# Vision tower on one core: the slot logits of both images in one block, the second half's statistics behind the scaled keys, the gate's second half in the third gap

## The chip, the cores and the metric

The kernel runs on one NeuronCore of a Trainium2 chip. The metric is the device time of one launch in microseconds, as the median of several launches. Everything is float32; many products are split by hand into a high and a low part of the faster 32-bit format and summed from three products.

## The reference

64 images of 224 x 224 x 3 are cut into 196 patches each and embedded into 192 features. Then come an attention without softmax and a mixture of 64 slot experts, each with a residual and a normalization:

```python
h = patches(x) @ W.T                                   # 64 x 196 x 192
q, k, v = silu(h @ Wq), silu(h @ Wk), silu(h @ Wv)     # 12 heads of 16
energy = (q @ k.T) * exp(log_slope * (n - m)) * (n >= m)
a = (energy @ v) * sigmoid(h @ Wg1 @ Wg2) @ Wo
h = layernorm(h + layernorm(a) * ln_w + ln_b)
xn = rms_norm(h) * norm_w
logits = (l2(slots) * scale) @ l2(xn).T                # 64 slots x 196 tokens
y = softmax_over_tokens(logits) @ xn                   # slot inputs
y = gelu(y @ fc1 + b1) @ fc2 + b2                      # each slot its own expert
out = layernorm(h + softmax_over_slots(logits).T @ y)
```

## The kernel before, in words

Images go through in 32 pairs (`NP`). Each engine has its own program, written out by hand; the order of its instructions is the order of the code, and semaphores join the engines. Three phases follow each other.

**Phase 1, the steps.** `step(i, c, d, e, f, more)` exists once for each engine and does four stages of four different pairs: embedding and attention of pair i; output product, first norm and residual of pair i-1 (flag c); second norm, scaled tokens, their transpose, logits and softmaxes of pair i-2 (d); slot inputs and combine weights of pair i-3 (e). Steps 4 to 30 are a hardware loop; 0 to 3 and 31 are written out. A pair is held as 4 token tiles of 98 rows: tiles 0 and 2 are the first halves of the two images, tiles 1 and 3 the second halves.

The attention of a step is a dialogue between TensorE and VectorE over four PSUM banks (2 to 5). TensorE's `scores(i, k)` (L1227) writes a third of the products of queries and keys; VectorE's `decay(i, k)` (L947) multiplies them by the decay into `p_sb` and frees the banks; only then can TensorE write the next third. `values(i, k)` (L1260) multiplies `p_sb` by the values. Between scores(0), scores(1), scores(2) and values(2) TensorE has three gaps, which hold other work: in the first, `token_features` (L1296, transposes of the scaled tokens `xn` of pair i-2, which must wait for `hb_sb` since they use the banks from which VectorE copies `hb`), `keys_turned` (L1234, L1235), `combine_turned` (L1289) and `slot_inputs_turned` (L1280, L1282); in the second, `gate` (L1173 and L1174: 128 features into bank 0, the other 64 into bank 1), `values(i, 0)`, `states` (L1243) and the logits of the first image of pair i-2; in the third, the logits of the second image, `values(i, 1)`, `carried` (L1274) and `logits_turned` (L1311). `logits(j, a)` (L1303) makes two products for image a: 96 rows, 64 columns of the array, those of slots 0 to 63 or 64 to 127 of the result. A float32 product is two records in the trace.

VectorE's order in a step (names of the helpers): gains and first norm of the first halves, `residual(i-1, 0)` (L883), `residual_statistics(i-1, 0)` (L889, L892), `cosine_scales`, then `first_norm`, `residual` and `residual_statistics` of the second halves, the low part of the gate's `zs` (L1011), `hb` (L1018: the turned h plus a bias), decay(0), the scaled keys `kts` (L1027), decay(1), `state` (L1033), decay(2), `gated(i, 0)` (L954: `og` from the gate's tanh and the PSUM sum), `slot_maxima` (`lneg`, L967), `shifted_logits` (L960, L962), `gated(i, 1)`, and the sums of the softmaxes.

ScalarE, after the SiLUs of keys, queries and values: the turned tokens `tokT` (L674), copies of the turned slot inputs and combine weights, the tanh of the gate's two parts (`gt`, L658 and L661), the rounding of the second half of the next x (`xh`, L597), a load of the exponential's table (L609), `logits_kept` (`Es`, L680), `slot_exponentials` (L710), `token_exponentials` (L715).

GpSimd: low parts of x and of the turned h (L440, L496), the powers of the norms, the scaled tokens `xn` (`unit_tokens`, L526), the scaled queries `qd`, the combine weights `Cn` (L533). The sync engine issues the loads and stores; after its last step it loads the weights of the first slots as soon as the memory under them is free.

**The passage** (`drain` on TensorE, the straight code behind `phase1` on the others) finishes pairs 29, 30 (`one`) and 31 (`last`): for each, token features, logits, transposes, softmaxes, slot inputs. It is a chain from engine to engine, and TensorE fills part of its waits with `idle_products(bank, count)` (L1129), products whose results nobody reads.

**Phase 2** runs 32 pairs of slots over six weight buffers; **phase 3** combines, adds the residual, normalizes and stores.

## Time and profile before

| | us |
|---|---|
| median of 3 runs | 1193.31 (1191.71 to 1193.66) |
| the profiled execution, its own time | 1190.01 |
| span of its trace | 1188.3 |
| TensorE busy in the span | 1076.5 (91%) |
| VectorE busy | 862.8 (73%) |
| ScalarE busy | 738.8 (62%) |
| GpSimd busy | 628.2 (53%) |
| mean granted TensorE clock | 0.954 of full speed |

Busy time of TensorE is modelled, since its products are pipelined: each record lasts until its result is written, while the next one already streams. What a product costs is thus read from the distance between the starts of neighbours, not from its own duration, and the share of busy time says little. The chain of waits is more use, and the timelines of all engines laid beside each other.

### The profile page before, as it was taken

What the parts mean: (1) busy time and instruction counts of PE and PEld (TensorE: products, weight loads), DVE (VectorE), ACT (ScalarE), POOL (GpSimd) and SP (SyncE); (2) the same over time, 40 slices, a digit from 0 to 9 for tenths busy, and PEclk for the clock granted to TensorE, in tenths of its full rate; (3) what the DMA queues carried; (4) which work ended last, traced back from release to release, by engine and by line L of the source; (5) the groups of instructions that cost most, each with busy time, mean ns of one, the idle gap of its engine ahead of it and who ended that gap; (6) DMA issues with size and microseconds to landing.
All of it is one profiled execution on the core that took longest, in us unless ns stands there. A gap on an engine that the chain in (4) does not pass through costs nothing.

```text
span 1188.3 us, 35236 instructions
## 1 busy us (share of the span) xinstructions
PE 1076.5 (91%) x13008; PEld 837.5 (70%) x13008; DVE 862.8 (73%) x2154; ACT 738.8 (62%) x1711; POOL 628.2 (53%) x967
## 2 busy tenths in 40 slices
PE   7799999999999999999999999999988999996653
PEld 6677788777777777877777778777765655554331
DVE  5878888888888888888888888888872222223996
ACT  6357777777777777777777777777753111110666
POOL 4556666666666665666666666566641000001664
PEclk9999999999999999999999999999999999998555
DMA  4511222111111122111111112211074999995885
GB/s 157 201 52 53 65 88 66 54 54 54 54 54 54 54 69 83 64 54 54 54 54 54 54 54 79 76 61 54 14 306 129 420 423 423 423 424 166 246 257 177
DMA packets 50994, 158.48 MB, mean 133 GB/s; under 512 B 5658, under 2 KB 31664, under 8 KB 38644
## 3 DMA queue, kind: packets, MB, share of 16 engines
q1 hardware_dynamic: 33352, 145.11, 33.3%
q10 hardware_dynamic: 17600, 12.78, 3.5%
q8 instruction: 30, 0.49, 0.2%
q14 instruction: 12, 0.10, 0.0%
HBM read 132.25 MB, written 25.62 MB: 133 GB/s over the span
## 4 chain that ended last, share of the span: by engine, by line
POOL 36%; issue 27%; PE 22%; DVE 10%; ACT 2%; DVEq 1%; DMA 1%; POOLq 1%; ACTq 0%; SPq 0%
POOL xl L440 14%; PE ps L1463 6%; POOL xn L526 5%; PE ps L1482 4%; POOL ra L517 4%; POOL hTl L496 4%; POOL rstd L507 2%; DVE res L1103 2%; POOL invn L500 2%; PE ps L1498 2%; DVE st L1109 2%; PE ps L1489 2%; POOL qd L477 1%; DVE p_sb L947 1%; PE ps L1227 1%
## 5 line engine op out<-in xcount | busy, mean ns | idle before, releaser
L947 DVE TENSOR_TENSOR p_sb<-ps,dec 98x1568 f32<-98x1568 f32 x96 | 171.6, 1788 | 64.2 <-PE ps L1227 64.1
L440 POOL TENSOR_TENSOR xl<-x_sb,xh 128x392 fp32r<-128x392 f32 x186 | 190.2, 1049 | 45.7 <-ACT xh L597 45.7
L496 POOL TENSOR_TENSOR hTl<-hT,hTh 128x392 fp32r<-128x392 f32 x64 | 66.3, 1035 | 146.3 <-ACT hTh L705 98.6
L763 ACT ACTIVATE hg<-ps 128x768 f32<-128x768 f32 x32 | 25.9, 810 | 144.3 <-PE ps L1489 144.3
L883 DVE SCALAR_TENSOR_TENSOR t<-t,rstd,hb 98x192 f32<-98x192 f32 x128 | 93.1, 767 | 15.9 <-POOL rstd L507 15.5
L1095 DVE COPY y2st<-ps 128x192 f32<-128x192 f32 x32 | 11.4, 357 | 120.5 <-PE ps L1463 120.5
L554 POOL CAST pickb<-pick 128x128 fp32r (+1 forms) x32 | 9.4, 293 | 150.4 <-PE ps L1489 150.4
L780 ACT ACTIVATE o_sb<-res,nb,rstd 98x192 f32<-98x192 f32 x128 | 59.6, 536 | 44.6 <-DVE nb L1118 44.0
L1260 PE MATMUL ps<-p_sb,vpad 98*32 98x98 f32 x3072 | 85.7, 252 | 1.5 <-DVE p_sb L947 1.5
L1260 PEld LDWEIGHTS ps<-p_sb,vpad 98*32 98x32 f32 x3072 | 64.7, 110 | 26.7 <-issue 26.7
L1513 PE MATMUL ps<-y2b,cbuf 64*98 64x192 f32 x256 | 49.4, 537 | 37.6 <-POOL y2b L567 37.6
L609 ACT ACT_TABLE_LOAD x60 | 77.0, 1283 | 1.1
L597 ACT ACTIVATE xh<-x_sb 128x1176 fp32r<-128x1176 f32 x64 | 75.4, 1180 | 1.9 <-DMA x_sb<-in_xT 1.2
L1133 PE MATMUL ps<-xl,wh 128*128 128x392 f32 x192 | 70.0, 365 | 3.4 <-POOL xl L444 3.3
L698 ACT ACTIVATE h<-t,mur,ra 98x192 f32<-98x192 f32 x128 | 59.7, 537 | 19.1 <-DVE mur L914 18.9
L1513 PEld LDWEIGHTS ps<-y2b,cbuf 64*98 64x98 f32 x256 | 32.6, 268 | 54.2 <-issue 43.0
L1463 PEld LDWEIGHTS ps<-w2v,hgT 128*64 128x64 f32 x768 | 52.3, 137 | 25.8 <-issue 18.5
L1463 PE MATMUL ps<-w2v,hgT 128*64 128x192 f32 x768 | 69.5, 330 | 1.0 <-DVE hgT L1089 1.0
L1227 PE MATMUL ps<-qA,kA 32*98 32x196 f32 x1024 | 59.6, 345 | 10.7 <-ACT vpad L686 7.5
L1211 PE MATMUL ps<-xl,whl 128*128 128x392 f32 x192 | 68.1, 355 | 0.0
L1133 PE MATMUL ps<-wvl,hTh 128*98 128x192 f32 x256 | 67.3, 263 | 0.2 <-DVE t L876 0.2
L533 POOL TENSOR_TENSOR Cn<-Ec,crec 98x256 f32<-98x256 f32 x32 | 20.6, 645 | 86.3 <-DVE crec L977 86.3
(228 smaller groups left out, 3449.0 us busy)
## 6 DMA issues: line engine op xcount, KB each, us to landing
x_sb<-in_xT SPq DMA_DIRECT2D x32, 1176.0 KB, 5.4
w1v<-in_fc SPq DMA_DIRECT2D x32, 1152.0 KB, 11.1
w2v<-in_fc SPq DMA_DIRECT2D x32, 1152.0 KB, 13.6
h_dram<-h SPq DMA_DIRECT2D x32, 294.0 KB
h2r<-h_dram SPq DMA_DIRECT2D x32, 294.0 KB
out<-o_sb ACTq DMA_DIRECT2D x32, 294.0 KB
comb_dram<-cst SPq DMA_DIRECT2D x32, 98.0 KB, 5.1
cbuf<-comb_dram SPq DMA_DIRECT2D x32, 98.0 KB, 3.8
```

The costliest lines, as they stand in the source:

```text
L440: pool.tensor_tensor(xl[:, k], x_sb[:, k], xh[:, k].bitcast(F32), ALU.subtract)\
L496: pool.tensor_tensor(hTl[:, k], hT[:, k], hTh[:, k].bitcast(F32), ALU.subtract).then_inc(hTl_rdy[k], 1)
L597: act.activation(xh[:, c], x_sb[:, c], ACT.Copy).then_inc(xh_rdy, 1)
L609: act.activation(warm[:, 1:2], warm[:, 0:1], func)
L883: dve.scalar_tensor_tensor(t2[0:T, t], t2[0:T, t], rstd1[:, t:t + 1], hb[0:T, t], ALU.mult, ALU.add).then_inc(t2_rdy, 1)
L947: dve.tensor_tensor(dst, src, rate.unsqueeze(2).to_broadcast([T, 4, 2, TOK]), ALU.mult)\
L1133: pe.matmul(out, hi, x_lo, start=start, stop=False)
L1211: pe.matmul(ps[:, 1, 0:PT], whl[:, k], xl[:, k], start=(k == 0), stop=False)
L1227: mm = pe.matmul(ps[0:T, SC_AT + r, mt * TOK:(mt + 1) * TOK].rearrange("p (b n) -> p b n", b=2), keys[rows, n], queries[rows, :, n], start ...
L1260: mm = pe.matmul(ps[32 * r:32 * r + 32, 6 + k // 2, at:at + T], vpad[:, 2 * a + mt, 32 * h:32 * h + 32], p_sb[:, k % 2, mt, (2 * r + odd) ...
L1463: mm = pe.matmul(ps[64 * s:64 * s + 64, 4 + n % 2, 0:D], hgT[:, k, at:at + 64], w2v[n][:, s, k], start=(k == 0), stop=(k == FJ - 1))
L1513: mm = pe.matmul(ps[0:T, 2 * n + a, k * D:(k + 1) * D], cbuf[64 * a:64 * a + 64, n, k * T:(k + 1) * T], y2b[64 * a:64 * a + 64, n, :], sta ...
```

## The change

Four things. In every step, TensorE makes both images' logits in one block in the second gap, the two images alternating; `lg_mm`, which releases ScalarE's copy, comes once, as before. The gate's second part moves from the second gap behind scores(2) into the third, and with it the waits for the bank that it writes. VectorE's statistics of the second halves move from ahead of `zs` and `hb` to behind the scaled keys. ScalarE's rounding of x and its copy of the logits now stand between the two tanh. In the passage, two of the four tiles of each pair's scaled tokens go to ScalarE (for `one`, beside GpSimd; for `last`, beside VectorE), several pieces change places, and the numbers of idle products change. The load of slot pair 2's weights waits for the gate instead of the scores.

```diff
@@ sync
             sp.wait_ge(qd_rdy, 2 * NP)
-            sp.wait_ge(sc_mm, 3 * NP)
+            sp.wait_ge(g_mm, 2 * NP)
             load_weights(2, 2)
@@ gpsimd
-            def unit_tokens(j):
+            def unit_tokens(j, tiles=range(4)):
...
-            unit_tokens(one)
+            unit_tokens(one, range(2))
@@ scalar, step
                 act.activation(gt[:, 0:PT], ps[:, 0, 0:PT], ACT.Tanh, scale=0.5).then_inc(g_sb, 1)
+                if more:
+                    round_x(i + 1, 1)
+                if d:
+                    logits_kept(i - 2)
                 act.wait_ge(g_mm, 2 * i + 2)
...
                 last.then_inc(g_sb, 1)
-                if more:
-                    round_x(i + 1, 1)
                 if d:
                     use_table(ACT.Exp)
-                    logits_kept(i - 2)
                     slot_exponentials(i - 2)
@@ scalar, passage
             combine_kept(one - 1, 1, True)
+            act.wait_ge(cosc_rdy, one + 1)
+            act.wait_ge(y_mm, one)
+            for t in range(2, 4):
+                act.activation(xn[0:T, t], gn[0:T, t], ACT.Copy, scale=cosc[:, t:t + 1]).then_inc(xn_rdy, 1)
             token_rows(one)
+            squares(last)
             logits_kept(one)
             slot_exponentials(one)
             token_exponentials(one)
-            squares(last)
+            act.wait_ge(cosc_rdy, NP)
+            for t in range(2, 4):
+                act.activation(hb[0:T, t], gn[0:T, t], ACT.Copy, scale=cosc[:, t:t + 1]).then_inc(xn_rdy, 1)
             slot_inputs_scaled(one)
             slot_inputs_kept(one, 5, 0)
             token_rows(last)
-            combine_kept(one, 4, True)
             logits_kept(last)
             slot_exponentials(last)
+            combine_kept(one, 4, True)
             token_exponentials(last)
@@ vector, step
                     residual(i - 1, 1)
-                    residual_statistics(i - 1, 1)
                 dve.wait_ge(zh_rdy, i + 1)
...
                                   ALU.mult).then_inc(kts_rdy, 1)
+                if c:
+                    residual_statistics(i - 1, 1)
                 decay(i, 1)
@@ vector, passage
+            cosine_scales(one, size)
             residual(last, 0)
-            cosine_scales(one, size)
             residual(last, 1)
...
             tokens(last)
+            token_norms(last)
             slot_maxima(one)
             shifted_logits(one)
             slot_sums(one)
-            token_norms(last)
+            cosine_scales(last, size_last)
             dispatch_scaled(one, size)
+            dve.wait_ge(cosc_rdy, NP)
+            for t in range(2):
+                dve.tensor_scalar(hb[0:T, t], gn[0:T, t], cosc[:, t:t + 1], None, ALU.mult).then_inc(xn_rdy, 1)
+            token_sums(one)
             mean_shifts(last)
-            token_sums(one)
-            cosine_scales(last, size_last)
-            dve.wait_ge(cosc_rdy, NP)
-            for t in range(4):
-                dve.tensor_scalar(hb[0:T, t], gn[0:T, t], cosc[:, t:t + 1], None, ALU.mult).then_inc(xn_rdy, 1)
@@ tensor
-            def logits(j, a):
+            def logits(j):
                 pe.wait_ge(tokT_sb, j + 1)
                 for k in range(2):
-                    mm = pe.matmul(ps[64 * a:64 * a + 64, 0, 0:TOK], slT[:, k, :], tokT[0:G, k, a * TOK:(a + 1) * TOK],
-                                   start=(k == 0), stop=(k == 1))
-                if a:
-                    mm.then_inc(lg_mm, 1)
+                    for a in range(2):
+                        mm = pe.matmul(ps[64 * a:64 * a + 64, 0, 0:TOK], slT[:, k, :],
+                                       tokT[0:G, k, a * TOK:(a + 1) * TOK], start=(k == 0), stop=(k == 1))
+                mm.then_inc(lg_mm, 1)
@@ tensor, step
                 pe.wait_ge(kts_rdy, i + 1)
+                gate(i, 0)
+                if d:
+                    pe.wait_ge(tokT_sb, i - 1)
+                values(i, 0)
+                states(i)
+                if d:
+                    pe.wait_ge(g_sb, 2 * i + 1)
+                    logits(i - 2)
+                scores(i, 2, c)
                 if e:
                     pe.wait_ge(yT_sb, 2 * i - 4)
                     pe.wait_ge(cb_sb, i - 2)
-                gate(i)
-                if d:
-                    pe.wait_ge(tokT_sb, i - 1)
-                values(i, 0)
-                states(i)
-                if d:
-                    pe.wait_ge(g_sb, 2 * i + 1)
-                    logits(i - 2, 0)
-                scores(i, 2, c)
-                if d:
-                    logits(i - 2, 1)
+                gate(i, 1)
                 carried_ready(i)
                 values(i, 1)
@@ tensor, drain
                 slot_inputs_turned(one, 5, 0)
+                idle_products(2, 2)
+                token_features(last, hb)
                 idle_products(2, 3)
-                token_features(last, hb)
-                idle_products(2, 4)
-                logits(last, 0)
-                logits(last, 1)
+                logits(last)
+                idle_products(2, 2)
                 combine_turned(one, 4)
                 pe.wait_ge(Lc_rdy, one + 1)
                 logits_turned(last)
-                idle_products(2, 6)
+                idle_products(2, 4)
                 dispatch_turned(last)
                 idle_products(2, 2)
                 slot_inputs(last, hb)
-                idle_products(2, 4)
+                idle_products(2, 3)
                 pe.wait_ge(yT_sb, 2 * last)
                 slot_inputs_turned(last, 5, 0)
-                idle_products(2, 6)
+                idle_products(2, 5)
```

TensorE's order in the loop, from scores(1) to values(2), before (L1227 scores, L1173 and L1174 gate, L1260 values, L1303 logits):

```order
L1227 MATMUL ps<-qA,kA 98x196 x8
L1381 REGISTER_ALU
L1173 MATMUL ps<-zs,gw 128x392
L1174 MATMUL ps<-zs,gw 64x392
L1260 MATMUL ps<-p_sb,vpad 32x98 x16
L1243 MATMUL ps<-vpad,kts 32x32 x12
L1303 MATMUL ps<-tokT,slT 64x196 x2
L1221 REGISTER_ALU
L1227 MATMUL ps<-qB,kB 98x196 x8
L1303 MATMUL ps<-tokT,slT 64x196 x2
L1260 MATMUL ps<-p_sb,vpad 32x98 x16
L1274 MATMUL ps<-qd,state 32x98 x8
```

The same stretch now (L1237 scores, L1184 gate, L1270 values, L1314 logits):

```order
L1237 MATMUL ps<-qA,kA 98x196 x8
L1184 MATMUL ps<-zs,gw 128x392
L1270 MATMUL ps<-p_sb,vpad 32x98 x16
L1253 MATMUL ps<-vpad,kts 32x32 x12
L1314 MATMUL ps<-tokT,slT 64x196 x4
L1231 REGISTER_ALU
L1237 MATMUL ps<-qB,kB 98x196 x8
L1400 REGISTER_ALU
L1184 MATMUL ps<-zs,gw 64x392
L1270 MATMUL ps<-p_sb,vpad 32x98 x16
L1284 MATMUL ps<-qd,state 32x98 x8
```

The second logits went up ahead of scores(2), the gate's part of 64 features went down behind it.

VectorE's order in the loop, from the second halves' residual to decay(1), before (L889 and L892 the statistics, L947 the decays):

```order
L883 SCALAR_TENSOR_TENSOR t<-t,rstd,hb 98x192 x2
L889 BN_STATS st<-t 98x6 x2
L892 BN_AGGR mv<-st 98x2 x2
L1011 TENSOR_TENSOR zs<-ps,zs 16x392
L1014 REGISTER_ALU
L1018 TENSOR_TENSOR hb<-ps,lnb 98x768
L942 ISA
L947 TENSOR_TENSOR p_sb<-ps,dec 98x4x2x196
L1027 TENSOR_TENSOR kts<-ps,kdec 98x384
L942 REGISTER_ALU
L947 TENSOR_TENSOR p_sb<-ps,dec 98x4x2x196
```

And now (L897 and L900 the statistics, L955 the decays):

```order
L891 SCALAR_TENSOR_TENSOR t<-t,rstd,hb 98x192 x2
L1018 TENSOR_TENSOR zs<-ps,zs 16x392
L1021 REGISTER_ALU
L1025 TENSOR_TENSOR hb<-ps,lnb 98x768
L950 ISA
L955 TENSOR_TENSOR p_sb<-ps,dec 98x4x2x196
L1034 TENSOR_TENSOR kts<-ps,kdec 98x384
L897 BN_STATS st<-t 98x6 x2
L900 BN_AGGR mv<-st 98x2 x2
L950 REGISTER_ALU
L955 TENSOR_TENSOR p_sb<-ps,dec 98x4x2x196
```

The statistics stand between the scaled keys and decay(1), where before nothing stood.

## Rows read from the trace of the kernel before

**Rows 1.** Stretches: us, busy us and instructions by engine, TensorE clock, DMA share, GB/s

```profile
60.00:866.00 806.00, 769.87 (x10335) 634.52 (x10334) 676.21 (x1612) 603.10 (x1425) 512.86 (x742) 1.00 0.17 58
866.00:912.00 46.00, 37.66 (x433) 28.93 (x433) 24.58 (x78) 21.62 (x63) 14.20 (x27) 0.96 0.59 229
```

**Rows 2.** Waits, 120 to 850 us: engine, line, releaser, us in all, times, longest

```profile
PE ps L1296 <- DVE hb L1018: 24.4, 27, 0.9
```

**Rows 3.** Timeline of TensorE in step 16: start, us, line, tiles, shape, count

```profile
459.26 0.92 PE L1227 MATMUL ps<-qA,kA 32*98 32x196 f32 x16 [0.23 <-ACT vpad L686]
...
462.78 0.92 PE L1227 MATMUL ps<-qA,kA 32*98 32x196 f32 x16
463.75 0.42 PE L1173 MATMUL ps<-zs,gw 80*128 80x392 f32 x1
...
464.27 0.89 PE L1260 MATMUL ps<-p_sb,vpad 98*32 98x98 f32 x32
...
465.28 0.88 PE L1303 MATMUL ps<-tokT,slT 96*64 96x196 f32 x4
466.08 0.92 PE L1227 MATMUL ps<-qB,kB 32*98 32x196 f32 x16
...
469.38 0.88 PE L1260 MATMUL ps<-p_sb,vpad 98*32 98x98 f32 x32
```

**Rows 4.** Timeline of VectorE in step 16; in brackets the idle time before

```profile
458.45 0.60 DVE L889 BATCH_NORM_STATS2 st<-t 98x6 f32<-98x192 f32 x2
459.13 0.25 DVE L892 BATCH_NORM_AGGREGATE mv<-st 98x2 f32<-98x6 f32 x2
...
460.88 1.78 DVE L947 TENSOR_TENSOR p_sb<-ps,dec 98x1568 f32<-98x1568 f32 x1
462.58 0.55 DVE L1027 TENSOR_TENSOR kts<-ps,kdec 98x384 f32<-98x384 f32 x1
463.77 1.79 DVE L947 TENSOR_TENSOR p_sb<-ps,dec 98x1568 f32<-98x1568 f32 x1 [0.64 <-PE ps L1227]
...
467.07 1.79 DVE L947 TENSOR_TENSOR p_sb<-ps,dec 98x1568 f32<-98x1568 f32 x1 [1.35 <-PE ps L1227]
469.17 0.56 DVE L954 SCALAR_TENSOR_TENSOR og<-gt,ps 128x392 f32<-128x392 f32 x1 [0.30 <-PE ps L1274]
```

**Rows 5.** Timeline of TensorE, last step and passage

```profile
863.57 0.92 PE L1227 MATMUL ps<-qA,kA 32*98 32x196 f32 x16 [0.23 <-ACT vpad L686]
...
872.91 0.89 PE L1260 MATMUL ps<-p_sb,vpad 98*32 98x98 f32 x32
...
885.08 0.88 PE L1296 MATMUL ps<-ident,xn 98*96 98x98 f32 x8 [2.98 <-POOL xn L526]
...
886.87 0.89 PE L1303 MATMUL ps<-tokT,slT 96*64 96x196 f32 x8
...
892.46 0.87 PE L1324 MATMUL ps<-xn,DT 98*64 98x192 f32 x8 [1.99 <-DVE DT L928]
...
896.18 1.28 PE L1296 MATMUL ps<-ident,hb 98*96 98x98 f32 x8
...
900.38 0.40 PE L1311 MATMUL ps<-ident,Es 128*98 128x128 f32 x2 [0.80 <-ACT Es L680]
```

**Rows 6.** Timeline of VectorE, last step and passage

```profile
864.55 1.79 DVE L947 TENSOR_TENSOR p_sb<-ps,dec 98x1568 f32<-98x1568 f32 x1
...
891.48 0.16 DVE L906 TENSOR_TENSOR nra<-ss,ra 98x4 f32<-98x4 f32 x1 [1.80 <-ACT ysq L691]
```

**Rows 7.** Timeline of ScalarE in step 16

```profile
464.66 0.65 ACT L661 ACTIVATE gt<-ps 64x196 f32<-64x196 f32 x2
465.34 1.18 ACT L597 ACTIVATE xh<-x_sb 128x1176 fp32r<-128x1176 f32 x1
466.54 1.28 ACT L609 ACT_TABLE_LOAD   x1
...
470.03 0.46 ACT L710 ACTIVATE Es<-Es,lneg 128x196 f32<-128x196 f32 x1 [1.78 <-DVE lneg L967]
```

More of the change, by code:

```diff
@@ L524, in unit_tokens @@
                     pool.wait_ge(y_mm, j)
-                for t in range(4):
+                for t in tiles:
                     pool.tensor_tensor(xn[0:T, t], gn[0:T, t], cosc[:, t:t + 1].to_broadcast([T, D]), ALU.mult)\
@@ L1070, in _ @@
             slot_sums(one)
-            token_norms(last)
+            cosine_scales(last, size_last)
             dispatch_scaled(one, size)
+            dve.wait_ge(cosc_rdy, NP)
+            for t in range(2):
+                dve.tensor_scalar(hb[0:T, t], gn[0:T, t], cosc[:, t:t + 1], None, ALU.mult).then_inc(xn_rdy, 1)
+            token_sums(one)
             mean_shifts(last)
-            token_sums(one)
-            cosine_scales(last, size_last)
-            dve.wait_ge(cosc_rdy, NP)
-            for t in range(4):
-                dve.tensor_scalar(hb[0:T, t], gn[0:T, t], cosc[:, t:t + 1], None, ALU.mult).then_inc(xn_rdy, 1)
             slot_maxima(last)
@@ L1168, in rows_of_v, with gate @@
                 mm.then_inc(v_mm, 1)
-            def gate(i):
-                pe.wait_ge(q_sb, 2 * i + 2)
-                pe.wait_ge(zl_rdy, i + 1)
-                pe.matmul(ps[:, 0, 0:PT], gw[:, 0:DA], zs[:, :], start=True, stop=True).then_inc(g_mm, 1)
-                pe.matmul(ps[0:DB, 1, 0:PT], gw[:, DA:D], zs[:, :], start=True, stop=True).then_inc(g_mm, 1)
+            def gate(i, g):
+                if g == 0:
+                    pe.wait_ge(q_sb, 2 * i + 2)
+                    pe.wait_ge(zl_rdy, i + 1)
+                m = (slice(0, DA), slice(DA, D))[g]
+                pe.matmul(ps[0:m.stop - m.start, g, 0:PT], gw[:, m], zs[:, :], start=True, stop=True).then_inc(g_mm, 1)
             def slots_turned():
@@ L1379, in step @@
                 pe.wait_ge(kts_rdy, i + 1)
-                if e:
-                    pe.wait_ge(yT_sb, 2 * i - 4)
-                    pe.wait_ge(cb_sb, i - 2)
-                gate(i)
+                gate(i, 0)
                 if d:
@@ L1389, in step @@
                     pe.wait_ge(g_sb, 2 * i + 1)
-                    logits(i - 2, 0)
+                    logits(i - 2)
                 scores(i, 2, c)
-                if d:
-                    logits(i - 2, 1)
+                if e:
+                    pe.wait_ge(yT_sb, 2 * i - 4)
+                    pe.wait_ge(cb_sb, i - 2)
+                gate(i, 1)
                 carried_ready(i)
@@ L1416, in drain @@
                 idle_products(0, 4)
-                logits(one, 0)
-                logits(one, 1)
+                logits(one)
                 pe.wait_ge(t1_rdy, 4 * NP)
```

## The prediction

> **What bounds the kernel now.** I read the stretches first [rows 1]. The pipelined steps (60 to 866 us) take two thirds of the time, and there TensorE has work in flight for 770 of 806 us; in the passage from the steps to the slot products (866 to 912) for only 38 of 46 us. A step takes 26.95 us: the first scores of two steps 15 apart start at 459.26 and 863.57 [rows 3, 5]. TensorE is thus nearly the bound of a step, but a row of the timeline hides stalls, so the waits come next [rows 2]: TensorE waits 0.9 us in each of 27 steps for `hb`, VectorE's copy of the turned h, before it can turn the token features.
>
> Then the timelines of one step. I follow the distance from the first scores, scores(0), to the last values product, values(2), since everything that the change touches in a step lies between them: 469.38 - 459.26 = 10.12 us [rows 3]. In that stretch TensorE and VectorE hand one PSUM area back and forth: scores(0), decay(0), scores(1), decay(1), scores(2), decay(2), values(2). A decay takes 1.79 us, starts 0.99 after its scores (466.08 to 467.07), and TensorE goes on 0.12 after its end (460.88 + 1.78 = 462.66, scores(1) at 462.78) [rows 3, 4]. Other products fill the three gaps. The reader should see two delays there. First, decay(0) starts 460.88 - 459.26 = 1.62 after scores(0), not 0.99, because `hb` and the statistics of the second half (458.45 to 459.38, 0.96 with the gap to the next instruction) stand ahead of it. Second, in the third gap TensorE is late, not VectorE: decay(2) ends at 467.07 + 1.79 = 468.86, values(2) could start at 468.98 and starts at 469.38 [rows 3, 4].
>
> The last step is a natural experiment. There VectorE is in time: decay(0) starts 864.55 - 863.57 = 0.98 after scores(0), and values(2) follows at 872.91 - 863.57 = 9.34 [rows 5, 6].
>
> **The statistics behind the scaled keys.** They leave the place ahead of decay(0), so I take the last step's 0.98: decay(0) starts 0.64 earlier, and the 0.9 us wait for `hb` goes, since `hb` would be written at about the time that the first scores end. scores(1) then starts at 0.98 + 1.79 + 0.12 = 2.89 after scores(0). What VectorE does not do there it does after the keys: 462.58 + 0.55, then 0.96, so decay(1) starts at about 464.1 instead of 463.77 on the old clock, in place of an idle time of 0.64 [rows 4]. It ends at 465.9 and TensorE may go on at 466.0.
>
> **The second gap.** On TensorE the gate's second half leaves (the pair takes 464.27 - 463.75 = 0.52, a half 0.26) and the second image's logits arrive. One image's logits take 466.08 - 465.28 = 0.80 [rows 3]. What do both take in one block? The passage shows it: eight records in 0.89, where one image's four take 0.88 [rows 3, 5]. So the second image costs nothing beside the first, and I take 0.80. The block then runs 465.02 to 465.82, just ahead of the 466.0 at which VectorE lets scores(2) start. From scores(1) to scores(2) it is 466.0 - 462.78 = 3.22, before 3.30. VectorE, no longer TensorE, ends this gap, by 0.2 us, and this is what is late next.
>
> The Trainium skill ("TensorE: Matmul & The Clock Gate", Part 3, the mechanism) says that a weight load overlaps a running matmul only when it targets other rows of the array. Both images' logits use the same 96 rows and differ in columns, so by that rule they would run one after the other. The row of the passage speaks against it, with eight records in the time of four. The same row says that the alternation itself is worth nothing: there the images already stand one after the other and still overlap.
>
> **The third gap.** TensorE loses 0.80 of logits and gains 0.26 of gate. values(2) is then bound by decay(2): 0.99 + 1.79 + 0.12 = 2.90 after scores(2), before 3.30. TensorE's own work there sums to 3.30 - 0.80 + 0.26 = 2.76, which fits by 0.14.
>
> The sum of a step: 2.89 + 3.22 + 2.90 = 9.01, against 10.12, so 1.11 saved. Of it goes 0.09: VectorE's gating, and with it all that feeds the next step (logits shifted, means, second norm), started 0.21 ahead of values(2) (469.17 and 469.38) and will start 0.12 ahead; that chain is the one that VectorE and ScalarE work through without idle time afterwards. Net 1.02. For 29 steps that is 29.6 us, and the last step, already at 9.34, gives 0.33. **Steps: -29.9 us.**
>
> ScalarE's side is costed at nothing. Its second tanh now waits for the gate half behind scores(2). On the old clock the half starts at 466.0 + 0.9; the tanh starts 0.65 after its half (463.75 + 0.26 and 464.66) and takes 0.65, so it ends near 468.2, and table load and warming, 1.5, end at 469.7 [rows 3, 7]. Today the exponential behind them waits 1.78 for `lneg` and starts at 470.03; with the gating at 468.8 instead of 469.17 it could start at 469.65. So this wait is the cover, and it shrinks to nothing. The rounding of x (1.18) moves ahead of the tanh, into the time in which scores(2) runs. On GpSimd the token scales wait for the moved statistics about 1 us longer; the second split of x behind them, which waits for ScalarE's rounding today, starts no later than now. No DMA of the steps is moved.
>
> **The passage.** Four pieces. (1) TensorE waited 2.98 for GpSimd's four scaled tiles [rows 5]; now it does two and ScalarE two, and the scales come ahead of the residuals. The first logits come 1.4 us earlier, but ScalarE's squares of the last pair now stand between them and their copy, and take back about 1.0. (2) VectorE waited 1.80 for those squares before it could scale the dispatch weights [rows 6]; they are now done before, and the slot inputs (892.46) come 1.8 earlier instead, which includes piece (1). (3) The last pair's token features started 3.72 after the slot inputs (896.18) [rows 5]; with the scaled rows written by two engines beforehand, no wait is left but that for the turned slot inputs, 2.4 us: -1.3. (4) From these features to the turned logits it takes 900.38 - 896.18 = 4.20, with a 0.80 wait for ScalarE's copy, which stood behind another pair's combine copy [rows 5]; without that copy in front, and with fewer idle products, 3.4: -0.8. Fewer idle products (4 for 6, 3 for 4, 5 for 6) free the last chain by another 0.9. Together -4.8 us; bounds are -2 (only piece 2) and -6.5 (if every removed idle product and every slow product counts). The weights for the first slots are asked for in the last step and land long before the passage ends, so the third one's new wait (for the gate instead of the scores) costs nothing; the slot products keep their pace and just begin earlier. **Passage: -4.8 us.**
>
> **The sum** against the profiled execution: 1190.01 - 29.9 - 4.8 = 1155.3 us. The median of the three runs, 1193.31, lies 3.3 above that execution; for a median I predict 1193.31 - 34.7 = 1158.6 us, a ratio of 0.971. A difference under 0.2% (2.4 us) I count as no change.
>
> **Rivals.**
> (a) *The tail binds.* The chain gating, shifted logits, exponential, means, second norm takes the place of the removed wait, because ScalarE's slack before its exponential is down to nothing and VectorE's tail has none. If it holds back half a microsecond of each step, 15 us are lost: 1173 us. For it: the small slacks above. Against: TensorE has the whole first embedding block between values(2) and the first product that needs the result. Chance 0.17.
> (b) *Both images' logits do not overlap in the loop.* The joined block takes 1.61. It ends at 466.63, scores(2) starts 0.55 later than now, values(2) at 9.65 instead of 10.12 after scores(0): 0.47 a step less the 0.09. 30 steps give 11, the passage 4.8: 1177 us. That is the time that the skill's rule on rows would give. Against it: the passage's row. Chance 0.05.
> (c) *More than forecast.* The chain from decay to values loses a little more in each gap, and the passage gives its upper bound: 1150 us. Chance 0.10.
> (d) *Slower.* The second tanh is the mechanism. It stands behind the rounding of x and behind the copy of the joined logits, and TensorE's turning of the logits waits for it, with values(2) queued behind in TensorE's order. TensorE comes to that turning at about 468.4, and with the 0.14 that its gap has to spare, the tanh may end 0.3 us later than the 468.2 worked out before values(2) is late. The 1.02 of a step and the passage's 4.8 (0.16 a step) are used up from 1.5 us on; at 2.0 us the kernel loses 30 x 0.5 = 15 us: 1208 us. For it: it is the one operation that moves 2 us later in the step. Against: the rounding needs 1.18 and the copy one short row, and both fit into the 2.9 us between its two tanh. Chance 0.03.
> (e) *It does not do what it says.* The alternation adds nothing (which I expect), and VectorE comes out as the end of the second gap, so that only the moved statistics pay: about 9.34 as in the last step, 0.78 a step, 1165 us. Chance 0.10.
>
> **How the numbers follow.** The forecast itself, 1154 to 1163, has 0.55. The likeliest case gives the time. The range leaves out (d), (b) and the ends of (a) and (c): 1151 to 1173. Faster by more than 0.2%: 0.96; within 0.2%: 0.01, out of (a) at twice its price; slower: 0.03, which is (d).
>
> **What would show it.** In the changed profile: no wait of the token features' turning for `hb`; decay(0), (1), (2) at 0.98, 4.2 and 7.1 us after scores(0); values(2) at 9.0; one block of eight logits records in 0.9 us; a step of 25.9 us; ScalarE's wait before the exponential down from 1.8 to a few tenths; the passage near 41 us; slot products and output untouched. Wrong would be a step above 26.3 us, a logits block of 1.6 us, or a new wait on `gt` ahead of TensorE's turning of the logits.

## The result, and the profile after

| | before | changed |
|---|---|---|
| median, us | 1192.51 (1189.90 to 1193.66, 4 runs) | 1144.17 (1142.75 to 1145.80, 4 runs) |
| profiled execution, its span | 1190.01, 1188.3 | 1145.80, 1144.0 |
| ratio | | 0.960, 95% interval 0.958 to 0.962 |

The change saves 48 us. I had forecast 35 us and a range of 1151 to 1173 us; the result is below the range.

One step of the changed kernel on TensorE, from the first scores (L1237) to those of the next step: L1306 token features, L1184 gate, L1270 values, L1314 logits. It answers to [rows 3]:

```profile
441.47 0.92 PE L1237 MATMUL ps<-qA,kA 32*98 32x196 f32 x16 [0.23 <-ACT vpad L687]
442.52 0.87 PE L1306 MATMUL ps<-ident,xn 98*96 98x98 f32 x8
...
444.29 0.92 PE L1237 MATMUL ps<-qA,kA 32*98 32x196 f32 x16
445.14 0.45 PE L1184 MATMUL ps<-zs,gw 80*128 80x392 f32 x1
445.52 0.89 PE L1270 MATMUL ps<-p_sb,vpad 98*32 98x98 f32 x32
...
446.52 0.88 PE L1314 MATMUL ps<-tokT,slT 96*64 96x196 f32 x8
447.34 0.92 PE L1237 MATMUL ps<-qB,kB 32*98 32x196 f32 x16
448.19 0.39 PE L1184 MATMUL ps<-zs,gw 80*64 80x392 f32 x1
448.51 0.89 PE L1270 MATMUL ps<-p_sb,vpad 98*32 98x98 f32 x32
...
450.17 0.89 PE L1270 MATMUL ps<-p_sb,vpad 98*32 98x98 f32 x32
...
466.99 0.92 PE L1237 MATMUL ps<-qA,kA 32*98 32x196 f32 x16 [0.23 <-ACT vpad L687]
```

VectorE in the same step, L1025 the copy `hb`, L955 the decays, L897 the moved statistics, L962 the gating. It answers to [rows 4]:

```profile
441.43 0.96 DVE L1025 TENSOR_TENSOR hb<-ps,lnb 98x768 f32<-98x768 f32 x1
442.45 1.79 DVE L955 TENSOR_TENSOR p_sb<-ps,dec 98x1568 f32<-98x1568 f32 x1
...
444.62 0.61 DVE L897 BATCH_NORM_STATS2 st<-t 98x6 f32<-98x192 f32 x2
...
445.47 1.77 DVE L955 TENSOR_TENSOR p_sb<-ps,dec 98x1568 f32<-98x1568 f32 x1
...
448.33 1.79 DVE L955 TENSOR_TENSOR p_sb<-ps,dec 98x1568 f32<-98x1568 f32 x1 [0.93 <-PE ps L1237]
450.03 0.55 DVE L962 SCALAR_TENSOR_TENSOR og<-gt,ps 128x392 f32<-128x392 f32 x1
```

A step is 25.52 us long (466.99 - 441.47), 1.42 less than before. The token features follow the scores with no wait for `hb`. From scores(0) it is 2.82 us to scores(1), 5.87 to scores(2) and 8.70 to values(2); before it was 3.52, 6.82 and 10.12. From values(2) to the next scores(0) it is 16.82 us, as before (26.95 - 10.12 = 16.83). So the whole gain of a step is where the change is.

The logits of both images take 0.82 us in one block of eight records (446.52 to 447.34). The two halves of the gate take 0.38 (445.14 to 445.52) and 0.32 (448.19 to 448.51) apart, where the pair took 0.52.

ScalarE's second tanh (L665) and the exponential (L711), in the same step:

```profile
448.62 0.67 ACT L665 ACTIVATE gt<-ps 64x196 f32<-64x196 f32 x2 [0.83 <-PE ps L1184]
...
450.89 0.46 ACT L711 ACTIVATE Es<-Es,lneg 128x196 f32<-128x196 f32 x1
```

The exponential no longer waits at all (no bracket; before 1.78 [rows 7]), and the second tanh waits 0.8 us for its half of the gate. Nobody waits for it.

The last step and the passage on TensorE, which answers to [rows 5]: first scores, values(2), slot inputs of `one`, token features and turned logits of `last`; below it ScalarE's first GELU.

```profile
824.36 0.92 PE L1237 MATMUL ps<-qA,kA 32*98 32x196 f32 x16 [0.24 <-ACT vpad L687]
...
833.23 0.89 PE L1270 MATMUL ps<-p_sb,vpad 98*32 98x98 f32 x32
...
851.18 0.87 PE L1334 MATMUL ps<-xn,DT 98*64 98x192 f32 x8
...
853.71 0.84 PE L1306 MATMUL ps<-ident,hb 98*96 98x98 f32 x8
...
856.99 0.38 PE L1321 MATMUL ps<-ident,Es 128*98 128x128 f32 x2
```

```profile
866.29 0.81 ACT L771 ACTIVATE hg<-ps 128x768 f32<-128x768 f32 x1
```

Counted from the last step's scores(0), before and now: values(2) at 9.34 and 8.87; slot inputs at 28.89 and 26.82; token features of `last` at 32.61 and 29.35; turned logits at 36.81 and 32.63; GELU at 47.0 and 41.9. From the GELU to the end it is 277.7 us in both traces. Of the 5.1 us gained up to the GELU, 0.47 are the last step's (9.34 and 8.87) and 4.6 the passage's.

Not all of these 4.6 us come from the order of the work. In the trace before, TensorE's granted clock was at half speed in one stretch of the passage (the columns are those of [rows 1]):

```profile
893.70:897.10 3.40, 3.40 (x20) 2.98 (x19) 1.07 (x6) 0.66 (x3) 0.01 (x1) 0.50 0.05 18
```

In the changed kernel's trace it is 1.00 from the last step to the GELU. What such a stretch costs can be estimated from c1_stats below, which has the passage of before and a second stretch of 3.4 us at 0.50 in it: its GELU comes 48.7 us after the last step's scores(0), against 47.0. By this estimate some 1.7 of the 4.6 us are the clock's. All three traces with the old passage have such a stretch ahead of the GELU (before, c1_stats, c2_logits), and none of the nine with the new one. So it may well be an effect of the change, but no run separates it from the rest.

The balance of the two traces: the 29 periods between the first scores of steps 2 and 31 took 781.2 us and take 740.6, 40.6 less; last step and passage 5.1 less; the start, up to the first scores of step 2, takes 1.4 us more (82.3 and 83.7). Together 44.3, the difference of the spans. The medians differ by 48.3, since the profiled execution of before was one of its fastest and that of the changed kernel its slowest.

### The profile page after: what moved, and what is told of

The parts are those of the page before. It is cut to its first block, busy times and chain, and to the rows that moved or that the text cites. A ratio compares the mean times of both kernels' runs of the same rounds, so it can differ in the third digit from the quotient of the medians.

```text
span 1144.0 us, 35221 instructions
## 1 busy us (share of the span) xinstructions
PE 1059.4 (93%) x13000; PEld 826.5 (72%) x13000; DVE 859.9 (75%) x2152; ACT 745.1 (65%) x1715; POOL 629.4 (55%) x965
## 4 chain that ended last, share of the span: by engine, by line
POOL 37%; issue 25%; PE 20%; DVE 10%; DMA 3%; ACT 1%; DVEq 1%; POOLq 1%; ACTq 0%; SPq 0%
POOL xl L440 14%; PE ps L1471 5%; POOL xn L526 5%; POOL hTl L496 4%; PE ps L1490 4%; POOL ra L517 3%; POOL rstd L507 3%; POOL invn L500 2%; DVE res L1112 2%; DVE st L1118 2%; DMA w2v<-in_fc 2%; PE ps L1506 2%; PE ps L1497 2%; POOL qd L477 1%; POOL qd L481 1%
## 5 line engine op out<-in xcount | busy, mean ns | idle before, releaser
L955 DVE TENSOR_TENSOR p_sb<-ps,dec 98x1568 f32<-98x1568 f32 x96 | 171.3, 1784 | 33.3 <-PE ps L1237 31.6
L1270 PE MATMUL ps<-p_sb,vpad 98*32 98x98 f32 x3072 | 86.9, 254 | 0.8 <-DVE p_sb L955 0.5
L1270 PEld LDWEIGHTS ps<-p_sb,vpad 98*32 98x32 f32 x3072 | 65.7, 111 | 19.8 <-issue 14.4
L1237 PE MATMUL ps<-qA,kA 32*98 32x196 f32 x1024 | 59.6, 345 | 11.3 <-ACT vpad L687 7.5
L1144 PE MATMUL ps<-xh,wh 128*128 128x392 f32 x192 | 66.5, 346 | 0.0
```

The costliest lines, as they stand in the source:

```text
L955: dve.tensor_tensor(dst, src, rate.unsqueeze(2).to_broadcast([T, 4, 2, TOK]), ALU.mult)\
L1144: return pe.matmul(out, hi, x_hi, start=False, stop=stop)
L1270: mm = pe.matmul(ps[32 * r:32 * r + 32, 6 + k // 2, at:at + T], vpad[:, 2 * a + mt, 32 * h:32 * h + 32], p_sb[:, k % 2, mt, (2 * r + odd) ...
```

## The experiments

All ratios are against the kernel before on the same chip in the same rounds (medians 1192.1 to 1192.5).

### The parts of the change one at a time

**c1_stats**, the kernel before with only the statistics moved:

```diff
                     residual(i - 1, 1)
-                    residual_statistics(i - 1, 1)
...
                                   ALU.mult).then_inc(kts_rdy, 1)
+                if c:
+                    residual_statistics(i - 1, 1)
```

> Kernel before with one part alone: the statistics of the second halves behind the scaled keys. Theory (TensorE's own work fills gaps two and three, VectorE's lateness only the first): scores(1) comes 2.82 us after scores(0) instead of 3.52, both later gaps stay at 3.30, values(2) at 9.42 instead of 10.12, a step of 26.25 us, the kernel 20 us faster (about 1172). Rival (the statistics cost VectorE what they gain, and the whole gain of the change is the logits): within 3 us of before. Rival (the statistics alone bring the last step's 9.34): 26.17 us a step, 1170.

Measured: 1170.00 us, ratio 0.981 (0.978 to 0.985). The scores and the last values of one step on TensorE:

```profile
447.27 0.92 PE L1228 MATMUL ps<-qA,kA 32*98 32x196 f32 x16 [0.24 <-ACT vpad L686]
...
450.10 0.92 PE L1228 MATMUL ps<-qA,kA 32*98 32x196 f32 x16
...
453.31 0.92 PE L1228 MATMUL ps<-qB,kB 32*98 32x196 f32 x16
...
456.62 0.88 PE L1261 MATMUL ps<-p_sb,vpad 98*32 98x98 f32 x32
```

values(2) comes 9.35 us after scores(0), and a step takes 26.17 us: 0.78 saved. That is the last step's distance in the kernel before [rows 5, 6], to a hundredth, as the last rival said, and not the 9.42 of my theory. The gap from scores(1) to scores(2) is 3.21 here, not 3.30, and the row of the gate says why:

```profile
450.97 0.43 PE L1174 MATMUL ps<-zs,gw 80*128 80x392 f32 x1
```

It starts 0.87 after scores(1), where before it started 0.97 after (463.75 and 462.78 [rows 3]). Ahead of the gate stand waits for ScalarE's copies of the turned slot inputs and combine weights; with the token features no longer late, these copies come in time. The last step had been the better witness than my sum.

**c2_logits**, everything of the steps but the statistics, with the passage of before:

```diff
@@ against the changed kernel: vector, step
                     residual(i - 1, 1)
+                    residual_statistics(i - 1, 1)
...
-                if c:
-                    residual_statistics(i - 1, 1)
@@ all engines: the passage as before
```

> The other part of the steps alone: logits in one block, gate's second half in the third gap, ScalarE's order as in the change; statistics and passage as before. Theory: the first gap stays (scores(1) at 3.52), the second takes 3.05, the third 2.83 as in the changed kernel, values(2) at 9.40, a step of 26.2 us, the kernel 21 us faster (about 1171); with the statistics' 0.70 this makes the 1.42 a step of the change. Rival (the two parts need each other, since the second gap is VectorE's): under 0.4 us a step, 1181 or more.

Measured: 1173.79 us, ratio 0.985 (0.981 to 0.988).

```profile
449.69 0.92 PE L1229 MATMUL ps<-qA,kA 32*98 32x196 f32 x16 [0.23 <-ACT vpad L687]
...
453.28 0.92 PE L1229 MATMUL ps<-qA,kA 32*98 32x196 f32 x16
...
456.32 0.92 PE L1229 MATMUL ps<-qB,kB 32*98 32x196 f32 x16
...
459.16 0.88 PE L1262 MATMUL ps<-p_sb,vpad 98*32 98x98 f32 x32
```

A step takes 26.29 us, 0.66 saved. The second gap is 3.04 and the third 2.84, as forecast; the first gap grew by 0.07, to 3.59. Both parts pay alone, and 0.78 + 0.66 = 1.44 comes close to the 1.42 of the change. That the sum fits so well is in part chance: the earlier start of the gate (0.10 in c1_stats, 0.12 here, where its waits have moved away) is in both parts and counts once in the change, while the 0.07 lost in the first gap is in this part only.

**c3_passage**, the steps of before with the passage of the change:

```diff
@@ pool, scalar, vector, tensor: the passage as in the change
-            unit_tokens(one)
+            unit_tokens(one, range(2))
...
```

> Steps of the kernel before, passage of the change. Theory: 4.6 us faster, all of it between the last step's values and the first GELU; steps untouched at 26.95 us. Rival (a part of the passage's gain needs the changed last step): 3 us or less.

Measured: 1185.85 us, ratio 0.994 (0.992 to 0.995). In the traces the steps keep 26.95 us and the first GELU comes 42.4 us after the last step's scores, before 47.0: 4.6 saved, as expected. The medians say 6.4, and the interval 5.6 to 9.5, while the two profiled executions differ by only 2.3 (1190.01 and 1187.73): in this one, the slowest of its kernel, the clock was at 0.51 from 907.0 to 910.4, just behind the GELU, and from the GELU to the end it took 280.1 us instead of 277.7. With such stretches at half speed in some executions and not in others, a difference of 1 to 2 us between medians and trace can't be placed. The medians of the three parts, 22.2 + 18.4 + 6.4 = 47.0, come near the 48.3 of the whole.

### What the alternation is worth

**c4_order**, the changed kernel with the images one after the other inside the block:

```diff
-                for k in range(2):
-                    for a in range(2):
+                for a in range(2):
+                    for k in range(2):
                         mm = pe.matmul(ps[64 * a:64 * a + 64, 0, 0:TOK], slT[:, k, :],
```

> The changed kernel with the logits of the two images one after the other inside the block, not alternating. Theory (the images overlap in either order, as they did in the passage before): the block stays at 0.82 us, the kernel within 1.5 us of the changed one (1144). Rival (only alternating neighbours overlap, the rule that a weight load overlaps a product only on other rows of the array): the block takes 1.2 to 1.6 us, 0.4 to 0.8 us a step, 1156 to 1168.

Measured: 1143.87 us, ratio 0.960 (0.956 to 0.963), the time of the changed kernel. The block of logits and the scores behind it:

```profile
442.31 0.89 PE L1314 MATMUL ps<-tokT,slT 96*64 96x196 f32 x8
443.13 0.92 PE L1237 MATMUL ps<-qB,kB 32*98 32x196 f32 x16
```

It takes 0.82 us in this order too. The gain comes from putting the images' logits side by side in the queue, whatever their order in it. Both use the same 96 rows of the array and different columns. So here four products, eight records, with their weight loads on two sets of columns take 0.82 us, where one image's two products, four records, took 0.80 [rows 3]. The weight loads of the changed kernel's block stand in its trace as one group:

```profile
446.52 0.53 PEld L1314 LDWEIGHTS ps<-tokT,slT 96*64 96x64 f32 x8
```

All eight fall into its first 0.53 us, while products of the block are running (446.52 to 447.34). The Trainium skill ("TensorE: Matmul & The Clock Gate", Part 3, the mechanism) says that a load overlaps running products only on other rows; the trace doesn't agree with that for these loads. The rule speaks of loads; that the two images' products would run one after the other was my own conclusion from it.

### Who ends the second and the third gap

**d1_gate**, the changed kernel with the gate's second half back in the second gap:

```diff
+                if e:
+                    pe.wait_ge(yT_sb, 2 * i - 4)
+                    pe.wait_ge(cb_sb, i - 2)
                 gate(i, 0)
+                gate(i, 1)
...
                 scores(i, 2, c)
-                if e:
-                    pe.wait_ge(yT_sb, 2 * i - 4)
-                    pe.wait_ge(cb_sb, i - 2)
-                gate(i, 1)
@@ sync
-            sp.wait_ge(g_mm, 2 * NP)
+            sp.wait_ge(sc_mm, 3 * NP)
             load_weights(2, 2)
```

> The changed kernel with the gate's second half back beside its first in the second gap (logits stay joined; the third slot pair's weights wait for the last scores again). The pair took 0.52 before, the two halves apart take 0.38 + 0.32. Theory (TensorE's work fills both gaps to the end): second gap 3.05 + 0.14 = 3.19, third gap VectorE's 2.83 as now, 0.14 us a step or 4 us slower (1148). Rival (VectorE ends the second gap with 0.1 to spare on TensorE): under 0.05 us a step, 1144 to 1145. Rival (the gap was TensorE's only and the third now gains): faster.

Measured: 1148.65 us, ratio 0.964 (0.961 to 0.967), 4.5 us above the changed kernel.

```profile
444.22 0.92 PE L1237 MATMUL ps<-qA,kA 32*98 32x196 f32 x16
...
447.44 0.92 PE L1237 MATMUL ps<-qB,kB 32*98 32x196 f32 x16
...
450.27 0.89 PE L1270 MATMUL ps<-p_sb,vpad 98*32 98x98 f32 x32 [0.27 <-DVE p_sb L955]
```

The second gap is 3.22, 0.17 longer than in the changed kernel: 0.14 is the pair's 0.52 in place of the first half's 0.38, and 0.03 the start of the gate, 0.88 after scores(1) behind the waits. The third stays at 2.83 with 0.32 us less work in it, and TensorE now waits 0.27 us for the decay. So more work of TensorE lengthens the second gap at once. In the third, VectorE allows no less than 2.83.

**d2_late**, two idle products in the third gap of steps 3 to 31:

```diff
                     pe.wait_ge(cb_sb, i - 2)
+                if e:
+                    idle_products(1, 2)
                 gate(i, 1)
```

> The changed kernel with two idle products of 128 columns ahead of the gate's second half in the third gap of steps 3 to 31; each took 0.22 to 0.25 us in the passage. Theory (the third gap is tied between TensorE's work and VectorE's decay, no slack on either): 0.45 us a step, 13 us slower (1157). Rival (VectorE's decay ends this gap with slack on TensorE, as predicted: 0.14): 0.3 us a step, 1153.

Measured: 1158.94 us, ratio 0.971 (0.968 to 0.974).

```profile
454.61 0.92 PE L1237 MATMUL ps<-qB,kB 32*98 32x196 f32 x16
455.46 0.71 PE L1138 MATMUL ps<-ident 128*128 128x128 f32 x4
455.93 0.42 PE L1184 MATMUL ps<-zs,gw 80*64 80x392 f32 x1
...
457.93 0.89 PE L1270 MATMUL ps<-p_sb,vpad 98*32 98x98 f32 x32
```

The products take 0.47 us, and the third gap grows from 2.83 to 3.32, a step by 0.49. TensorE has no slack in the third gap either. With d1_gate: there both engines arrive at the same time.

**d3_state**, the statistics one place further back, and GpSimd's split of x ahead of its token scales:

```diff
@@ vector
-                if c:
-                    residual_statistics(i - 1, 1)
                 decay(i, 1)
...
                                   ALU.mult).then_inc(s_sb, 1)
+                if c:
+                    residual_statistics(i - 1, 1)
@@ gpsimd
+                if more:
+                    split_x(i + 1, range(KP // 2, KP))
                 if c:
                     token_scales(i - 1)
-                if more:
-                    split_x(i + 1, range(KP // 2, KP))
```

> The changed kernel with the statistics one place further back, behind the states in VectorE's idle 0.93 us ahead of decay(2); GpSimd's second split of x goes ahead of the token scales so that it does not wait for them. decay(1) then starts about 0.2 us earlier, at 3.8. Theory (TensorE's own work fills the second gap too, scores 0.85, gate 0.38, values 0.70, states 0.30, logits 0.82 = 3.05): scores(2) and values(2) stay at 5.87 and 8.70, no gain, within 1.5 us of 1144. Rival (VectorE ends the second gap, as predicted): up to 0.2 us a step, 1138.

Measured: 1146.34 us, ratio 0.962 (0.959 to 0.964). VectorE's decay(1), then TensorE's scores(1) and scores(2):

```profile
444.72 1.79 DVE L955 TENSOR_TENSOR p_sb<-ps,dec 98x1568 f32<-98x1568 f32 x1 [0.58 <-PE ps L1237]
```

```profile
443.73 0.92 PE L1237 MATMUL ps<-qA,kA 32*98 32x196 f32 x16
...
446.78 0.92 PE L1237 MATMUL ps<-qB,kB 32*98 32x196 f32 x16
```

decay(1) starts 0.99 after scores(1), where in the changed kernel it starts 1.18 after, so VectorE is 0.19 us earlier. scores(2) still comes 3.05 after scores(1), and a step takes 25.52 us. The rival that VectorE ends the second gap falls. The median is 2.2 us above the changed kernel's, where I had expected 1.5 at most; the traces show no cause (29 periods of 740.5 us, the same passage), and I leave it open.

### The start, and a version that beats both

In the changed kernel the start took longer, not shorter. TensorE's stretches there (us, busy us and instructions of PE, PEld, DVE, ACT and POOL, granted clock, DMA share, GB/s), first before, then changed:

```profile
56.00:60.00 4.00, 2.41 (x20) 1.62 (x21) 2.70 (x4) 0.00 (x0) 2.50 (x5) 0.68 0.03 6
60.00:64.00 4.00, 4.00 (x74) 2.83 (x74) 1.88 (x2) 2.23 (x4) 1.18 (x2) 0.50 0.00 0
64.00:68.00 4.00, 3.30 (x96) 2.67 (x93) 2.86 (x5) 0.74 (x2) 1.79 (x2) 0.97 0.32 78
```

```profile
56.00:60.00 4.00, 3.06 (x41) 2.18 (x45) 3.47 (x7) 0.69 (x2) 1.72 (x4) 0.59 0.03 6
60.00:64.00 4.00, 4.00 (x86) 3.05 (x78) 2.00 (x3) 1.56 (x3) 3.46 (x4) 0.50 0.00 0
...
68.00:72.00 4.00, 4.00 (x18) 3.99 (x18) 1.86 (x6) 1.88 (x5) 0.00 (x0) 0.70 0.35 116
```

Both kernels fall from 2.4 to 1.2 GHz between 56 and 60 us, in step 1, where TensorE waits for VectorE twice (in the changed kernel 1.37 us before the turned keys and 1.16 before scores(1)). Before, the clock was back near 64 us; in the changed kernel's profile only near 70, and the first scores of step 2 come later for it.

**d4_warm** and, the same kernel again in five rounds beside the changed one, **e1_again** and **e2_warm**:

```diff
                 keys_turned(i)
+                if isinstance(i, int) and i == 1:
+                    idle_products(6, 4)
```

> The changed kernel with four idle products in step 1 behind the turned keys, where TensorE waits 1.16 us for VectorE's decay. In the changed kernel's trace TensorE's clock falls to 1.2 GHz near 57 us, after two idle times of 1.4 and 1.2 us, and is back only near 70; in the kernel before it was back near 64, and this costs the changed kernel 1.4 us between the first scores of steps 0 and 2. Theory (the clock follows that idle time): the clock stays up or is back sooner, 1 to 5 us faster than the changed kernel. Rival (it falls because of the earlier wait for hb, and the products come too late): within 1 us.

> The changed kernel once more, on the same chip and in the same rounds as the next one. 1144 us; the first scores of step 2 between 79 and 85 us, the place depending on how long TensorE's clock stays at 1.2 GHz in step 1.

> The changed kernel with the four idle products of step 1 (the same kernel as d4_warm), against e1_again. Theory (they keep the clock up over step 1): 2 to 5 us faster than e1_again, steps and passage the same, the first scores of step 2 near 79 us, the clock at full speed over step 1. Rival (the first result was a lucky start): within 1 us of e1_again.

Measured: d4_warm 1140.72 us, ratio 0.957 (0.954 to 0.959); e1_again 1145.11 us, ratio 0.958 (0.955 to 0.962); e2_warm 1140.48 us, ratio 0.956 (0.953 to 0.959). In the shared rounds the four idle products bring 4.6 us. The executions of e1_again run from 1140.9 to 1146.5 and those of e2_warm from 1139.1 to 1143.2, so this is a gain of the typical run and not of every one. TensorE in step 1 of e2_warm (the turned keys, the idle products, scores(1)) and two of the stretches above:

```profile
54.13 0.42 PE L1244 MATMUL ps<-ident,kA 128*98 128x128 f32 x2 [1.35 <-DVE hb L1025]
...
54.50 1.06 PE L1138 MATMUL ps<-ident 128*128 128x128 f32 x8
55.83 0.92 PE L1237 MATMUL ps<-qA,kA 32*98 32x196 f32 x16 [0.27 <-DVE p_sb L955]
```

```profile
56.00:60.00 4.00, 3.31 (x92) 2.30 (x88) 2.98 (x8) 1.57 (x2) 2.67 (x4) 1.00 0.00 0
60.00:64.00 4.00, 3.54 (x95) 2.90 (x95) 3.07 (x6) 1.73 (x5) 2.32 (x3) 1.00 0.22 39
```

The wait before scores(1) is down to 0.27 us, and the clock stays at full speed. The first scores of step 2 start at 77.96 us; in e1_again's profile, whose clock was at half speed to about 71 us, they start at 84.85. Steps and passage are those of the changed kernel in both. This is the fastest version of the study.

## Why the prediction was right or wrong

**Right: where.** The wait for `hb` went, the logits block cost one image's time, the alternation was worth nothing, decay(0) comes at 0.98, the slot products and the output did not move, and the passage with the last step gave 5.1 us where I had 0.33 + 4.8. Its inner marks fit too: slot inputs 2.1 earlier (forecast 0.33 + 1.8), last token features 3.3 (3.4), turned logits 4.2 (4.2). In the last two there is luck. The 3.72 and 4.20 us that pieces (3) and (4) start from both include time at half clock (the stretch from 893.7 to 897.1), and the changed kernel has none there. I had the slow products only in the upper bound of the passage; without the clock's 1.7 us, which is an estimate, the passage would have gained about 2.9. The reason inside piece (2) fits only in part: the squares are done in time, but VectorE then waits 1.33 us for GpSimd's token scales.

**Wrong: "The sum of a step: 2.89 + 3.22 + 2.90 = 9.01 ... Net 1.02".** It is 2.82 + 3.05 + 2.83 = 8.70 and nothing to take off, net 1.42. Over 29 steps the 0.40 are 11.6 us, and the miss against the medians is 14.4 us (1158.6 and 1144.17). Of the other 2.8 us, 0.8 is the median of before, which came out at 1192.51 and not 1193.31; the rest is within what executions of one kernel differ by. The step that failed was VectorE's side of the dialogue: each decay and its handover were costed too long, so that VectorE seemed to end the second gap, and 0.09 was taken off that never came due. The first of its four parts needs one more row of VectorE in step 16 of the kernel before, the one ahead of decay(0):

```profile
460.01 0.96 DVE L1018 TENSOR_TENSOR hb<-ps,lnb 98x768 f32<-98x768 f32 x1
```

1. *The handovers.* I added a decay's duration (1.79) and a latency (0.12) from decay(0) in step 16. There the decay's row begins while VectorE is still finishing `hb`: the row above ends at 460.97, and the decay's starts at 460.88 [rows 4]. A row can start before its predecessor ends. So the 1.90 from there to scores(1) (462.78) hold some of `hb`'s time. From start to start a decay that is not queued takes 1.84 (442.45 to 444.29), not 1.91. The last step showed it (decay(0) at 864.55 [rows 6], its scores(1) at 866.39), and I used that step for its other distances only. It enters the first and the third gap: 0.14 a step. It also takes 0.07 of the 0.14 of slack that I gave TensorE in the third gap; the other 0.07 is TensorE's own work, 2.83 and not 2.76, mostly the half gate at 0.32 and not 0.26. d2_late found no slack.
2. *The statistics after the keys.* I summed 0.55 and 0.96, both with an overlap counted twice. In place they put decay(1) 3.02 after decay(0), not 3.21. VectorE would thus let scores(2) start 3.02 after scores(1) (3.02 from decay to decay, the same handover at both ends), not 3.22, and was no longer the later one.
3. *The second gap's owner.* "VectorE, no longer TensorE, ends this gap, by 0.2 us" fell with d3_state: it is TensorE's own work, 0.85 + 0.38 + 0.70 + 0.30 + 0.82 = 3.05. My sum for TensorE there was right to 0.01 (465.82 - 462.78 = 3.04), by two errors that cancel. I had half the gate at 0.26, since I halved the pair; it takes 0.38. And I let the gate start 0.97 after scores(1) as before [rows 3], where now it starts 0.85 after: the old one stood behind the waits for ScalarE's copies of the turned slot inputs and combine weights. Either part of the change brings nearly all of this: with the statistics moved and the waits in place it is 0.87 (c1_stats) and 0.88 (d1_gate), since the copies come earlier; with the waits moved and the statistics in place it is 0.85 (c2_logits). Items 2 and 3 are the 0.17 of this gap (3.22 and 3.05).
4. *The 0.09 of the tail.* Gating now starts 0.14 ahead of values(2), before 0.21, so that chain does come later, and where the statistics stay in their old place it costs what I had feared: in c2_logits decay(0) comes 1.69 after scores(0), before 1.62, and the first gap grows by 0.07. In the changed kernel `hb` ends at 442.39 (441.43 + 0.96) and decay(0) starts at 442.45, in its usual 0.98 after the scores. VectorE is in time there with about 0.06 to spare, so the shift is covered and nothing was to be taken off.

So rivals (a), (b) and (d) did not occur: no wait took the old one's place, and the tanh that moved 2 us later held back nobody. Rival (e) was half right, on the alternation. Rival (c) named the side and said that the chain from decay to values would lose a little more in each gap, which is how it came; but it put no size on that, and at 1150 us it was too timid. A bound of the sum should have come from adding the small terms with the other sign, and I let the range's lower end rest on (c) instead. That TensorE and VectorE would come out even in two gaps of three I had not seen.

**Not in the prediction: the start.** I had taken it as unchanged; it took 1.4 us more in the profiled execution, in which the clock stayed at half speed longer, and it moves by some microseconds from one profile to the next.

## What to carry to other kernels

Cost a dialogue of two engines from start to start, taken from a place where the engine was not queued, and not from durations plus a latency: here handovers of 0.07 us too much and overlaps counted twice made most of 0.40 us a step, and over 29 steps a third of the predicted gain. If some step of the old kernel already runs under the new conditions, take its distances whole; the last step gave the statistics' effect to 0.01 us. Put small products that use the same rows and different columns of the array next to each other in TensorE's queue: the second image's two products of 196 columns cost 0.02 us beside the first's, in either order. But ask also which gap has room for a piece: the gate's halves, which use the same columns, take 0.18 us more of TensorE apart than as a pair (0.38 + 0.32 and 0.52), and yet the kernel is 4.5 us slower with the pair back together (d1_gate), since the third gap can't use the time. Before crediting a reordering with a gain, compare the granted clock of the two stretches: by my estimate one 3.4 us stretch at half speed in the old passage was a third of what the passage gained.

## What I had not expected of the hardware

The clock of TensorE differs between executions of one kernel, and the time goes with it. In the six executions of e1_again the mean granted clock was 0.954 and 0.955 where the kernel took 1140.92 and 1141.53 us, and 0.950 to 0.952 where it took 1144.50 to 1146.50. In the traces one such place is step 1: it falls to 1.2 GHz there after idle times of 1.2 to 2.2 us, and is back after about 7 us in some profiles and about 14 in others. The first scores of step 2 start at 79.5, 83.7 and 84.9 us in three profiles of kernels with the same start (c4_order, with 7 us at half speed; the changed one and e1_again, with 14), and at 78.7 and 78.0 in the two with the idle products, whose clock did not fall there. Which stretch made the executions without a profile slow isn't on record, and what else than the idle time decides how long the clock stays down was not tried.
